# The first attention's step: two phases of scores and values in place of four, with chains laid over two steps

## The chip, the cores and the metric

The kernel runs on one core of a Trainium2 chip. The metric is the device time of one execution in microseconds (us). TensorE (PE in the rows, PEld for its weight loads), VectorE (DVE), ScalarE (ACT), GpSimd (POOL) and SyncE (SP) each run their own instruction stream and wait for each other by semaphores. TensorE writes into PSUM, eight banks of 128 partitions x 512 fp32 numbers; VectorE and ScalarE read it; GpSimd works on SBUF alone.

## What is computed

Four blocks in a row, each with a residual and a layer norm: an attention over a compressed key and value, a mixture of experts, a second attention, and two layers of local attention with a feed-forward part. The change touches only the first block:

```python
def _L0_attn_ref(x, wq, w_kv_down, w_k_up, w_v_up, wo):     # x: (4, 512, 128)
    q = jnp.einsum('bsd,qd->bsq', x, wq).reshape(B, S, H, D).transpose(0, 2, 1, 3)   # H=16, D=64
    kv_latent = jnp.einsum('bsd,ld->bsl', x, w_kv_down)     # 64 numbers a token
    k = jnp.einsum('bsl,ql->bsq', kv_latent, w_k_up)...
    v = jnp.einsum('bsl,ql->bsq', kv_latent, w_v_up)...
    q = q * cos + _rotate_half(q) * sin
    k = k * cos + _rotate_half(k) * sin
    scores = jnp.einsum('bhsd,bhtd->bhst', q, k) / jnp.sqrt(jnp.float32(D))
    scores = scores + causal
    probs = jax.nn.softmax(scores, axis=-1)
    out = jnp.einsum('bhst,bhtd->bhsd', probs, v)
    return jnp.einsum('bsq,dq->bsd', out.transpose(0, 2, 1, 3).reshape(B, S, H * D), wo)
```

All of it is fp32.

## The kernel before

`attention0` goes through 32 steps, n = 0 to 31. A step is one pair of heads (8 pairs, the outer loop) on one batch of 512 tokens (4 batches, the inner one). The first four and the last four steps are written out, the 24 between run in a hardware loop of four steps (`each`). There is no scheduler: each engine's order is the order in which its `step` function issues, and what is in flight is ordered by counting semaphores.

Within a step a *phase* p = 0 to 3 stands for one block of 128 queries, from the last (p = 0) to the first (p = 3). By causality it has (4 - p) x 128 keys, `width(p)`: 512, 384, 256 and 128. j = 0, 1 is the head of the pair. In a phase:

- `scores` (TensorE, L478): one product for each head, K = 64 rows of queries, written to one of three rotating PSUM banks 1 to 3. An fp32 product is run as two passes, so two heads are four matmuls in the trace; the two heads lie on different rows of the array and run side by side.
- `rowmax` (VectorE, L382): mask, copy to `prob` and row minimum of the negated scores, then `exp` (ScalarE, L305) in place, with the row sum in `den`.
- `turn_p` (TensorE, L488): (4 - p) transposes for each head, into bank 4 (head 0) and bank 5 (head 1), then `copy_pT`: VectorE (L388) copies bank 4 and ScalarE (L311) copies bank 5 into `probT`. A copy is as wide as its phase.
- `values` (TensorE, L500): `lat` (the latents, 64 columns) times `probT`, accumulated into `o_ps`, bank 6; the two heads lie on different columns of the array.

Once a step there is also: `project` for w = 0, 1 (TensorE, L457: the next step's queries and keys, into bank 0), `rope` for each (VectorE, L369 and L372), `rope_sum` for each (GpSimd, L265), `turn_qk` for each (TensorE, L468, bank 0) and `copy_qkT` (ScalarE, L298), whose results the next step's `scores` read. And for the step before: `copy_o` (ScalarE, L316), `reciprocal` (VectorE), `widen` (GpSimd, L271), `spread` (TensorE, L511, turns the reciprocals into bank 7), `normalise` (VectorE, L399), `output` (TensorE, L518, bank 7) and `add_y` (VectorE, L405).

TensorE thus changes between three shapes of products in every phase: 64 rows x 128 columns (scores), 128 x 64 (values) and 128 x 128 (all others; the rows of the trace show them as `64*128`, `128*64` and `128*128`).

Of the kernel before, what the change touches and what calls it, by code (L numbers as in the profile page):

```python
# [129 lines left out]
def attention0(nc, ctx, io, keep):  # L130
# [34 lines left out]
    prob = sb("prob", [P, 4, S])  # L165
    probT = sb("probT", [P, 2, S])
# [27 lines left out]
    pT_mm = sem("pT_mm")  # L194
    pT_ev = [sem(f"pT_ev{j}") for j in range(2)]
    o_mm = sem("o_mm")
# [32 lines left out]
    def score_ps(b, p, j):  # L229

        return ps[:, 1 + (NU * b + 2 * p + j) % 3, :]
# [27 lines left out]
    def _(pool):  # L259
# [31 lines left out]
    def _(act):  # L291
# [65 lines left out]
    def _(dve):  # L357
# [6 lines left out]
        def rope(n, w):  # L364
            h = HD0 // 2
            src = qk_ps.rearrange("p (t g d) -> p t g d", t=TPB, d=HD0)
# [46 lines left out]
        def step(n, b, final):  # L413
# [3 lines left out]
            if later(n):  # L417
                copy_pT(n - 1, 3)
# [8 lines left out]
            if not final:  # L427
                rope(n + 1, 1)
# [2548 lines left out]
```

## Time and profile before

| | us |
|---|---|
| three runs before, median (lowest, highest) | 1637.8 (1637.06, 1641.13) |
| the profiled execution: its own time | 1635.31 |
| its span | 1633.2 |
| step 0 begins (first scores) | 22.70 |
| step 1 begins | 40.47 |
| step 31 begins | 435.38 |
| PE busy over the span | 1504.0 |
| DVE, ACT, POOL busy over the span | 1146.4, 1087.7, 523.0 |

The profiled execution lies 2.5 us under the median of the runs, and 2.1 us of its time lie outside its span. The first attention takes about the first 454 us of the 1633. A step of it repeats every 13.18 us inside the loop. A busy time of PE is the time in which some matmul is in flight; matmuls are pipelined, so the starts of two groups tell more than their lengths.

### The profile page before, as it was taken

The page shows a single profiled execution, that of the slowest core. Times are in us where ns is not written, and L with a number is a line of the kernel's source. Part 1 is how long each engine was busy: PE and PEld are TensorE (multiplying, and loading weights), DVE is VectorE, ACT ScalarE, POOL GpSimd, SP SyncE. Part 2 cuts the span into 40 slices and gives each one's busy share as a digit, 9 for nine tenths or more (in the row PEclk, how much of TensorE's full clock was granted, in tenths as well). Part 3 has the DMA queues.
Part 4 walks back from the last instruction along what each step waited for, and adds up shares of the span by engine and source line. Part 5 has one row for each costly group of instructions (what it writes and reads, how often), then busy time and mean ns, then how long its engine had stood idle before and what let it go on. Part 6 is the DMA issues. An engine that isn't in the chain of part 4 may idle for free. (4 is left out here: it accounts for less than half of the span.)

```text
span 1633.2 us, 30449 instructions
## 1 busy us (share of the span) xinstructions
PE 1504.0 (92%) x9934; PEld 1018.6 (62%) x9934; DVE 1146.4 (70%) x2592; ACT 1087.7 (67%) x2499; POOL 523.0 (32%) x476
## 2 busy tenths in 40 slices
PE   7999999999979999999998999997999988999986
PEld 6777777777657888888863333333666655566654
DVE  2677777676657777777787888864777753777755
ACT  3565665656567888888865777754778754787852
POOL 1222222222231122221110000014777733677732
PEclk9999999999979999999997999977999998999998
DMA  7000000000002212212100000000000000000000
GB/s 244 2 2 1 0 0 0 0 0 0 1 28 80 78 64 77 76 52 77 65 1 1 1 1 1 1 1 0 2 1 1 1 1 0 1 2 1 1 1 26
DMA packets 18849, 36.54 MB, mean 22 GB/s; under 512 B 5492, under 2 KB 10736, under 8 KB 16560
## 3 DMA queue, kind: packets, MB, share of 16 engines
q1 hardware_dynamic: 18752, 35.29, 6.4%
q8 instruction: 56, 0.92, 0.2%
q14 instruction: 41, 0.34, 0.1%
HBM read 34.10 MB, written 1.18 MB: 22 GB/s over the span
## 5 line engine op out<-in xcount | busy, mean ns | idle before, releaser
L915 DVE TENSOR_TENSOR m_hidp<-m_hid,m_hidp 128x512 fp32r<-128x512 f32 x256 | 178.2, 722 | 77.9 <-ACT m_hidp L831 76.6
L305 ACT ACTIVATE a_prob<-a_prob,a_negmax 128x512 f32<-128x512 f32 (+3 forms) x256 | 142.2, 556 | 135.9 <-DVE a_negmax L382 135.9
L836 ACT ACTIVATE m_hid<-ps,pre_w 128x512 f32<-128x512 f32 x256 | 175.3, 685 | 63.5 <-PE ps L1064 62.7
L1064 PE MATMUL ps<-c_sb_st,m_w1p 128*128 128x512 f32 x768 | 191.4, 398 | 0.0
L1119 PE MATMUL ps<-m_hidp,m_w2p 128*128 128x512 f32 x768 | 190.0, 396 | 0.2 <-DVE m_hidp L915 0.2
L1441 ACT ACTIVATE c_sb_pT<-ps 128x512 f32<-128x512 f32 x256 | 137.4, 601 | 70.7 <-PE ps L1654 69.7
L265 POOL TENSOR_TENSOR a_qk_r<-a_qk_c,a_qk_s 128x512 f32<-128x512 f32 x64 | 81.6, 1275 | 318.6 <-DVE a_qk_s L372 318.6
L1511 DVE TENSOR_REDUCE c_sb_negmax<-ps 128x1 f32<-128x512 f32 x240 | 152.5, 685 | 38.9 <-PE ps L1639 38.9
L1064 PEld LDWEIGHTS ps<-c_sb_st,m_w1p 128*128 128x128 f32 x768 | 144.7, 189 | 37.9 <-issue 3.0
L1119 PEld LDWEIGHTS ps<-m_hidp,m_w2p 128*128 128x128 f32 x768 | 144.1, 188 | 35.8 <-DVE m_hidp L915 0.4
L2038 ACT ACTIVATE l_sb_prob<-ps,l_sb_negmax,l_sb_rn 128x192 f32<-128x192 f32 (+1 forms) x256 | 124.1, 499 | 47.9 <-DVE l_sb_negmax L2140 47.9
L831 ACT ACTIVATE m_hidp<-m_hid 128x512 fp32r<-128x512 f32 x256 | 153.9, 630 | 0.0
L382 DVE CUSTOM_DVE_ANT_0 a_prob<-ps,a_cmask 128x512 f32<-128x512 f32 (+3 forms) x256 | 116.6, 486 | 24.1 <-PE ps L478 23.4
L1949 POOL TENSOR_TENSOR c_sb_pT<-c_sb_pT,l_sb_tab_s 128x512 f32<-128x512 f32 x64 | 110.5, 1748 | 19.6 <-ACT c_sb_pT L1996 16.8
L388 DVE COPY a_probT<-ps 128x512 f32<-128x512 f32 (+3 forms) x128 | 61.2, 478 | 78.9 <-PE ps L488 78.9
L500 PE MATMUL ps<-a_probT,a_lat 128*64 128x128 f32 x1280 | 98.2, 282 | 19.7 <-issue 17.2
L500 PEld LDWEIGHTS ps<-a_probT,a_lat 128*64 128x64 f32 x1280 | 68.3, 136 | 76.4 <-issue 47.6
L478 PE MATMUL ps<-a_qkT 64*128 64x256 f32 (+3 forms) x512 | 104.6, 485 | 1.1 <-ACT a_qkT L298 1.1
L488 PE MATMUL ps<-keep_ident,a_prob 128*128 128x128 f32 x640 | 96.1, 281 | 0.0
L1639 PE MATMUL ps<-c_sb_st 32*128 32x512 f32 x240 | 83.5, 518 | 10.4 <-ACT c_sb_pT L1441 10.4
L2135 DVE TENSOR_REDUCE ps<-ps 128x2 f32<-128x384 f32 (+1 forms) x128 | 67.4, 526 | 33.1 <-PE ps L2267 33.1
L759 POOL CAST m_w1p<-pre_w 128x512 fp32r<-128x512 f32 x16 | 9.8, 612 | 244.8 <-DMA pre_w<-w1T 181.0
(246 smaller groups left out, 3198.5 us busy)
## 6 DMA issues: line engine op xcount, KB each, us to landing
m_gate_all<-m_gates_d SPq DMA_DIRECT2D x16, 1024.0 KB, 4.6
pre_w<-w1T SPq DMA_DIRECT2D x14, 258.0 KB, 2.7
pre_w<-w2T SPq DMA_DIRECT2D x14, 256.0 KB, 2.8
pre_wqkv<-wqkv SPq DMA_DIRECT2D x2, 768.0 KB
keep_x<-x SPq DMA_DIRECT2D x1, 1024.0 KB, 9.4
out<-keep_x SPq DMA_DIRECT2D x4, 256.0 KB, 2.3
keep_xT<-xT SPq DMA_DIRECT2D x1, 768.0 KB, 6.8
pre_m_w<-l_w SPq DMA_DIRECT2D x2, 341.0 KB
```

Of the source, the lines that this page charges most:

```text
L305: nc.scalar.activation(prob[:, u % 4, 0:width(p)], prob[:, u % 4, 0:width(p)], ACT.Exp, scale=-1.0, bias=negmax[:, u:u + 1], accum_out=den ...
L382: nc.vector.tensor_tensor_reduce(prob[:, u % 4, 0:width(p)], score_ps(b, p, j)[:, 0:width(p)], cmask[:, S - width(p):S], 1.0, HUGE, ALU.ad ...
L500: ins = nc.tensor.matmul(o_ps[64 * j:64 * j + 64, i * P:(i + 1) * P], lat[:, b * TPB + t, :], probT[:, j, t * P:(t + 1) * P], start=(t == ...
L831: nc.scalar.activation(hidp[:, c % 2, 0, f, :], hid[:, c % 2, f, :], ACT.Copy).then_inc(high_done, 1)
L836: nc.scalar.activation(hid[:, c % 2, f, :], ps[:, f, :], ACT.Gelu, bias=w1[:, k, FF + f:FF + f + 1]).then_inc(gelu_done, 1)
L915: nc.vector.tensor_tensor(hidp[:, c % 2, 1, f, :], hid[:, c % 2, f, :], hidp[:, c % 2, 0, f, :], ALU.subtract).then_inc(low_done, 1)
L1064: ins = nc.tensor.matmul(ps[:, f, :], w1p[:, k, a, f * P:(f + 1) * P], xp[:, b, c, :], start=(i == 0), stop=(i == 2))
L1119: ins = nc.tensor.matmul(ps[:, 4 + c % 2, :], w2p[:, k, a, f, :], hidp[:, c % 2, b, f, :], start=(f == 0 and i == 0), stop=(f == FB - 1 an ...
L1441: nc.scalar.activation(pT[:, m % 2, g + i, t, :], ps[:, pair(exp_turn(e)).start + i, :], ACT.Exp, scale=SCALE).then_inc(exp_done, 1)
L1511: nc.vector.tensor_reduce(negmax[:, m % 2, t, g + i:g + i + 1], ps[:, pair(max_turn(k)).start + i, :], AX.X, ALU.max, negate=True).then_in ...
L1949: ins = nc.gpsimd.tensor_tensor(qk_s[:, :, :].rearrange("p w (g d) -> p w g d", d=HD2)[:, :, :, a:a + h], raw[:, :, :, h - a:2 * h - a], t ...
L2038: ins = nc.scalar.activation(prob[:, k % 2, keys(t, i)], ps[:, 2 + k % 2, keys(t, i)], ACT.Exp, bias=negmax[:, u:u + 1], scale=rn[:, t, u: ...
```

## The change

Two phases are put together where there were four. Phases 0 and 2 (512 and 256 keys) make one, phases 1 and 3 (384 and 128 keys, together the 512 columns of a bank) the other. TensorE now issues scores 0 and 2 back to back, then the values 0 and 2 of the step before, the turned probabilities 1 and 3 of the step before, both projections, scores 1 and 3, and the values 1 and 3 of the step before. The turned probabilities of a step are copied in five full banks instead of eight pieces: VectorE copies two (`copy_wide`, `copy_mix`), ScalarE three (`copy_wide`, `copy_mix`, and `copy_tail`, which holds phase 2 of both heads). All values of a step are now taken in the next step, `add_y` comes two steps later, and both projections have a bank of their own (0 and 7). `prob` and `probT` are split in two tiles each, with more room. The number of products, transposes, exponentials and rowmaxes is as before.

```diff
@@ -226,9 +231,48 @@
         return (TPB - p) * P
-    def score_ps(b, p, j):
-        return ps[:, 1 + (NU * b + 2 * p + j) % 3, :]
+    def two_on(n):
+        return not isinstance(n, int) or n > 1
+    def turn_of(p, j):
+        return {0: 0, 2: 2, 1: 4, 3: 6}[p] + j
+    def score_ps(p, j):
+        if p == 2:
+            return ps[:, 3 - 3 * j, 0:width(2)]
+        c = 0 if p == 0 else (p // 2) * width(1)
+        return ps[:, 1 + j, c:c + width(p)]
+    def prob_of(p, j):
+        if p % 2 == 0:
+            c = (p // 2) * S
+            return prob_a[:, j, c:c + width(p)]
+        c = (p // 2) * width(1)
+        return prob_b[:, j, c:c + width(p)]
+    def turned_ps(p, j):
+        if p == 2:
+            return ps[:, 3, j * 256:(j + 1) * 256]
+        c = 0 if p == 0 else (p // 2) * width(1)
+        return ps[:, 4 + j, c:c + width(p)]
+    def probT_of(p, j):
+        if p == 2:
+            return probT_a[:, 2, j * 256:(j + 1) * 256]
+        if p == 0:
+            return probT_a[:, j, :]
+        c = (p // 2) * width(1)
+        return probT_b[:, j, c:c + width(p)]
+    def proj_ps(w):
+        return m_ps if w else qk_ps
     @block.sync
     def _(sp):
...
@@ -277,11 +321,10 @@
         pool.wait_ge(ones_set, 1)
         def step(n, b, final):
-            if not final:
-                rope_sum(n + 1, 0)
             if later(n):
                 widen(n - 1)
             if not final:
+                rope_sum(n + 1, 0)
                 rope_sum(n + 1, 1)
         each(pool, step)
...
@@ -320,37 +371,34 @@
         def step(n, b, final):
             exp(n, b, 0, 0)
+            exp(n, b, 0, 1)
+            exp(n, b, 2, 0)
+            exp(n, b, 2, 1)
             if later(n):
-                copy_pT(n - 1, 3)
-            exp(n, b, 0, 1)
-            if not later(n):
+                copy_mix(n - 1)
+            else:
                 act.wait_ge(lat_mm, 1)
                 nc.scalar.activation(lat[:, :, :], ps[:, 4:6, :].rearrange("p a (t l) -> p (a t) l", l=LAT), ACT.Copy
                                      ).then_inc(lat_ev, 1)
                 act.wait_ge(set_mm, 2)
                 nc.scalar.activation(wvo[:, :, :], ps[:, 6:8, :].rearrange("p a (h n) -> p (a h) n", n=P),
                                      ACT.Copy).then_inc(set_ev, 1)
-            exp(n, b, 1, 0)
             if later(n):
                 copy_o(n - 1)
-            exp(n, b, 1, 1)
-            copy_pT(n, 0)
-            exp(n, b, 2, 0)
-            exp(n, b, 2, 1)
-            copy_pT(n, 1)
             if not final:
                 copy_qkT(n + 1, b + 1, 0)
+            exp(n, b, 1, 0)
+            copy_wide(n)
+            if not final:
+                copy_qkT(n + 1, b + 1, 1)
+            exp(n, b, 1, 1)
+            copy_tail(n)
             exp(n, b, 3, 0)
             exp(n, b, 3, 1)
-            if not final:
-                copy_qkT(n + 1, b + 1, 1)
-            copy_pT(n, 2)
         each(act, step)
-        copy_pT(NI - 1, 3)
+        copy_mix(NI - 1)
         copy_o(NI - 1)
     @block.vector
...
@@ -411,37 +462,31 @@
         dve.wait_ge(const_ld, 32)
         def step(n, b, final):
-            before = (b - 1) % NB
-            rowmax(n, b, 0, 0)
-            rowmax(n, b, 0, 1)
+            if two_on(n):
+                add_y(n - 2, (b - 2) % NB)
+            rowmax(n, 0, 0)
+            rowmax(n, 0, 1)
+            rowmax(n, 2, 0)
+            rowmax(n, 2, 1)
             if later(n):
-                copy_pT(n - 1, 3)
+                reciprocal(n - 1, (b - 1) % NB)
+                copy_mix(n - 1)
             if not final:
                 rope(n + 1, 0)
-            rowmax(n, b, 1, 0)
-            rowmax(n, b, 1, 1)
-            if later(n):
-                reciprocal(n - 1, before)
-            copy_pT(n, 0)
-            if not final:
                 rope(n + 1, 1)
-            rowmax(n, b, 2, 0)
-            rowmax(n, b, 2, 1)
-            copy_pT(n, 1)
+            rowmax(n, 1, 0)
+            rowmax(n, 1, 1)
+            copy_wide(n)
             if later(n):
                 normalise(n - 1)
-            rowmax(n, b, 3, 0)
-            rowmax(n, b, 3, 1)
-            copy_pT(n, 2)
-            if later(n):
-                add_y(n - 1, before)
+            rowmax(n, 3, 0)
+            rowmax(n, 3, 1)
         each(dve, step)
-        copy_pT(NI - 1, 3)
+        add_y(NI - 2, NB - 2)
         reciprocal(NI - 1, NB - 1)
+        copy_mix(NI - 1)
         normalise(NI - 1)
         add_y(NI - 1, NB - 1)
@@ -449,18 +494,17 @@
     def _(pe):
         def project(n, b, w):
             if w:
-                pe.wait_ge(rope_mul, 2 * n + 1)
+                wait_past(pe, y_add, n - 2)
             else:
-                wait_past(pe, qkT_ev, 2 * n)
+                wait_past(pe, max_done, NU * (n - 1) + 4)
             h = n // NB
             for t in range(TPB):
-                ins = nc.tensor.matmul(qk_ps[:, t * P:(t + 1) * P], xT[:, b, t * P:(t + 1) * P],
+                ins = nc.tensor.matmul(proj_ps(w)[:, t * P:(t + 1) * P], xT[:, b, t * P:(t + 1) * P],
                                        wqk[:, bass.ds(h, 1), w * P:(w + 1) * P].rearrange("p a n -> p (a n)"),
                                        start=True, stop=True)
             ins.then_inc(qk_mm, 1)
         def turn_qk(n, w):
-            pe.wait_ge(rope_mul, 2 * n + 2)
             pe.wait_ge(rope_add, 2 * n + w + 1)
             if w:
                 pe.wait_ge(qkT_ev, 2 * n + 1)
@@ -470,43 +514,66 @@
         def scores(n, b, p):
             i = TPB - 1 - p
-            wait_past(pe, max_done, NU * n + 2 * p - (0 if b == 0 and p == 0 else 1))
             if p == 0:
                 pe.wait_ge(qkT_ev, 2 * n + 2)
+                wait_past(pe, max_done, NU * n)
+            if p == 2:
+                wait_past(pe, tail_ev, n)
+            if p == 1:
+                pe.wait_ge(max_done, NU * n + 2)
             for j in range(2):
                 r = slice(64 * j, 64 * j + 64)
-                nc.tensor.matmul(score_ps(b, p, j)[:, 0:width(p)], qkT[r, b % 2, 0, i * P:(i + 1) * P],
+                nc.tensor.matmul(score_ps(p, j), qkT[r, b % 2, 0, i * P:(i + 1) * P],
                                  qkT[r, b % 2, 1, 0:width(p)], start=True, stop=True, skip_group_check=True
                                  ).then_inc(s_mm, 1)
-        def turn_p(n, p):
+        def turn(n, p, j):
+            pe.wait_ge(exp_done, NU * n + turn_of(p, j) + 1)
+            for t in range(TPB - p):
+                ins = nc.tensor.transpose(turned_ps(p, j)[:, t * P:(t + 1) * P],
+                                          prob_of(p, j)[:, t * P:(t + 1) * P], ident[:, :])
+            return ins
+        def turn_wide(n):
             for j in range(2):
-                u = 2 * p + j
-                pe.wait_ge(exp_done, NU * n + u + 1)
-                wait_past(pe, pT_ev[j], 4 * n + p)
-                for t in range(TPB - p):
-                    ins = nc.tensor.transpose(ps[:, 4 + j, t * P:(t + 1) * P], prob[:, u % 4, t * P:(t + 1) * P],
-                                              ident[:, :])
-                ins.then_inc(pT_mm, 1)
+                wait_past(pe, pT_ev[j], 2 * n)
+                turn(n, 0, j).then_inc(pT_wide, 1)
+        def turn_tail(n):
+            turn(n, 2, 0)
+            turn(n, 2, 1).then_inc(pT_tail, 1)
+        def turn_mix(n):
+            for j in range(2):
+                pe.wait_ge(pT_ev[j], 2 * n + 1)
+                turn(n, 1, j)
+                turn(n, 3, j).then_inc(pT_mix, 1)
         def values(n, b, p):
             i = TPB - 1 - p
-            for j in range(2):
-                pe.wait_ge(pT_ev[j], 4 * n + p + 1)
             if p == 0:
                 wait_past(pe, o_ev, n)
+                for j in range(2):
+                    pe.wait_ge(pT_ev[j], 2 * n + 1)
+            if p == 2:
+                pe.wait_ge(tail_ev, n + 1)
+            if p == 1:
+                for j in range(2):
+                    pe.wait_ge(pT_ev[j], 2 * n + 2)
             for t in range(i + 1):
                 for j in range(2):
                     ins = nc.tensor.matmul(o_ps[64 * j:64 * j + 64, i * P:(i + 1) * P], lat[:, b * TPB + t, :],
-                                           probT[:, j, t * P:(t + 1) * P], start=(t == 0), stop=(t == i),
+                                           probT_of(p, j)[:, t * P:(t + 1) * P], start=(t == 0), stop=(t == i),
                                            skip_group_check=True)
             if p == 3:
                 ins.then_inc(o_mm, 1)
-        def spread(n):
+        def spread(n, projected):
             pe.wait_ge(r_wide, n + 1)
             wait_past(pe, y_add, n)
+            if projected:
+                pe.wait_ge(rope_mul, 2 * n + 6)
             for t in range(TPB):
                 ins = nc.tensor.transpose(m_ps[:, t * P:(t + 1) * P], rden_x[:, t * P:(t + 1) * P], ident[:, :])
             ins.then_inc(r_mm, 1)
@@ -558,47 +625,47 @@
         def step(n, b, final):
             scores(n, b, 0)
+            scores(n, b, 2)
             if later(n):
+                values(n - 1, (b - 1) % NB, 0)
                 values(n - 1, (b - 1) % NB, 2)
-                turn_p(n - 1, 3)
+                turn_mix(n - 1)
             else:
                 latents(3)
+                pe.wait_ge(rope_mul, 2)
                 value_weights()
             if not final:
                 project(n + 1, (b + 1) % NB, 0)
+                if not later(n):
+                    pe.wait_ge(set_ev, 2)
+                project(n + 1, (b + 1) % NB, 1)
             scores(n, b, 1)
+            scores(n, b, 3)
             if later(n):
+                values(n - 1, (b - 1) % NB, 1)
                 values(n - 1, (b - 1) % NB, 3)
             else:
                 pe.wait_ge(lat_ev, 1)
-            turn_p(n, 0)
-            if not final:
-                project(n + 1, (b + 1) % NB, 1)
-            scores(n, b, 2)
-            if isinstance(n, int) and n == 0:
-                pe.wait_ge(set_ev, 2)
-            values(n, b, 0)
-            turn_p(n, 1)
             if not final:
                 turn_qk(n + 1, 0)
+            turn_wide(n)
             if later(n):
-                spread(n - 1)
-            scores(n, b, 3)
-            values(n, b, 1)
+                spread(n - 1, not final)
             if not final:
                 turn_qk(n + 1, 1)
+            turn_tail(n)
             if later(n):
                 output(n - 1)
-            turn_p(n, 2)
         each(pe, step)
+        values(NI - 1, NB - 1, 0)
         values(NI - 1, NB - 1, 2)
-        turn_p(NI - 1, 3)
+        turn_mix(NI - 1)
+        values(NI - 1, NB - 1, 1)
         values(NI - 1, NB - 1, 3)
-        spread(NI - 1)
+        spread(NI - 1, False)
         output(NI - 1)
```

The first place is TensorE from scores 0 on, in a step that is written out (L numbers are those of each file). Before:

```order
L478 MATMUL ps<-a_qkT 128x512 x2
L500 MATMUL ps<-a_probT,a_lat 64x128 x4
L488 MATMUL ps<-keep_ident,a_prob 128x128 x2
L457 MATMUL ps<-a_wqk,keep_xT 128x128 x4
L478 MATMUL ps<-a_qkT 128x384 x2
L500 MATMUL ps<-a_probT,a_lat 64x128 x2
L488 MATMUL ps<-keep_ident,a_prob 128x128 x8
L457 MATMUL ps<-a_wqk,keep_xT 128x128 x4
L478 MATMUL ps<-a_qkT 128x256 x2
L500 MATMUL ps<-a_probT,a_lat 64x128 x8
```

In the change the same stretch reads (L526 are scores, L565 values, L533 turned probabilities, L502 projections, L512 turned queries and keys, L578 the spread reciprocals, L585 the output):

```order
L526 MATMUL ps<-a_qkT 128x512 x2
L526 MATMUL ps<-a_qkT 128x256 x2
L565 MATMUL ps<-a_probT_a,a_lat 64x128 x12
L533 MATMUL ps<-keep_ident,a_prob_b 128x128 x8
L502 MATMUL ps<-a_wqk,keep_xT 128x128 x8
L526 MATMUL ps<-a_qkT 128x384 x2
L526 MATMUL ps<-a_qkT 128x128 x2
L565 MATMUL ps<-a_probT_b,a_lat 64x128 x8
L512 MATMUL ps<-keep_ident,a_qk_r 128x128 x4
L533 MATMUL ps<-keep_ident,a_prob_a 128x128 x8
L578 MATMUL ps<-keep_ident,a_rden_x 128x128 x4
L512 MATMUL ps<-keep_ident,a_qk_r 128x128 x4
```

Scores and values now stand in two groups a step, and no values of the running step are left in it.

The second place is ScalarE over one step that is written out. Before (L305 exponentials, L316 `copy_o`, L311 turned probabilities, L298 queries and keys):

```order
L305 ACTIVATE a_prob,a_den<-a_prob,a_negmax 128x512
L305 ACTIVATE a_prob,a_den<-a_prob,a_negmax 128x384
L316 ACTIVATE a_o_sb<-ps 128x512
L305 ACTIVATE a_prob,a_den<-a_prob,a_negmax 128x384
L311 ACTIVATE a_probT<-ps 128x512
L305 ACTIVATE a_prob,a_den<-a_prob,a_negmax 128x256 x2
L311 ACTIVATE a_probT<-ps 128x384
L298 ACTIVATE a_qkT<-ps 128x512
L305 ACTIVATE a_prob,a_den<-a_prob,a_negmax 128x128 x2
L298 ACTIVATE a_qkT<-ps 128x512
L311 ACTIVATE a_probT<-ps 128x256
```

And in the change (L348 exponentials, L362 `copy_mix`, L367 `copy_o`, L341 queries and keys, L354 `copy_wide`, L358 `copy_tail`):

```order
L348 ACTIVATE a_prob_a,a_den<-a_prob_a,a_negmax 128x512 x2
L348 ACTIVATE a_prob_a,a_den<-a_prob_a,a_negmax 128x256 x2
L362 ACTIVATE a_probT_b<-ps 128x512
L367 ACTIVATE a_o_sb<-ps 128x512
L341 ACTIVATE a_qkT<-ps 128x512
L348 ACTIVATE a_prob_b,a_den<-a_prob_b,a_negmax 128x384
L354 ACTIVATE a_probT_a<-ps 128x512
L341 ACTIVATE a_qkT<-ps 128x512
L348 ACTIVATE a_prob_b,a_den<-a_prob_b,a_negmax 128x384
L358 ACTIVATE a_probT_a<-ps 128x512
L348 ACTIVATE a_prob_b,a_den<-a_prob_b,a_negmax 128x128 x2
```

Behind the exponentials of phases 0 and 2, `copy_o` of the step before now stands ahead of everything else that ScalarE has to do in the step.

## Rows read from the trace of the kernel before

**Rows 1.** Windows: stretch, length, busy time of each engine (instructions), clock, DMA.
```profile
40.47:435.38 394.91, 377.68 (x3361) 285.92 (x3361) 277.64 (x869) 237.86 (x690) 106.53 (x90) 1.00 0.00 1
22.70:40.47 17.77, 16.99 (x126) 13.05 (x127) 7.68 (x25) 8.98 (x23) 2.56 (x2) 1.00 0.62 215
```

**Rows 2.** Timeline of PE, one step: start, length, line, out<-in, xcount, idle.
```profile
211.56 1.13 PE L478 MATMUL ps<-a_qkT 64*128 64x512 f32 x4
212.62 0.66 PE L500 MATMUL ps<-a_probT,a_lat 128*64 128x128 f32 x8
213.21 0.44 PE L488 MATMUL ps<-keep_ident,a_prob 128*128 128x128 f32 x2
213.48 1.06 PE L457 MATMUL ps<-a_wqk,keep_xT 128*128 x8
214.47 0.92 PE L478 MATMUL ps<-a_qkT 64*128 64x384 f32 x4
215.31 0.44 PE L500 MATMUL ps<-a_probT,a_lat 128*64 128x128 f32 x4
215.68 1.09 PE L488 MATMUL ps<-keep_ident,a_prob 128*128 128x128 f32 x8
216.61 1.06 PE L457 MATMUL ps<-a_wqk,keep_xT 128*128 x8
217.60 0.70 PE L478 MATMUL ps<-a_qkT 64*128 64x256 f32 x4
218.89 1.09 PE L500 MATMUL ps<-a_probT,a_lat 128*64 128x128 f32 x16 [0.59 <-issue]
219.92 0.88 PE L488 MATMUL ps<-keep_ident,a_prob 128*128 128x128 f32 x6
220.63 0.60 PE L468 MATMUL ps<-keep_ident,a_qk_r 128*128 128x128 f32 x4
221.07 0.60 PE L511 MATMUL ps<-keep_ident,a_rden_x 128*128 128x128 f32 x4
221.60 0.49 PE L478 MATMUL ps<-a_qkT 64*128 64x128 f32 x4
222.02 0.88 PE L500 MATMUL ps<-a_probT,a_lat 128*64 128x128 f32 x12
222.82 0.66 PE L468 MATMUL ps<-keep_ident,a_qk_r 128*128 128x128 f32 x4
223.32 1.06 PE L518 MATMUL ps<-a_wvo,a_oT 128*128 x8
224.21 0.60 PE L488 MATMUL ps<-keep_ident,a_prob 128*128 128x128 f32 x4
224.74 1.13 PE L478 MATMUL ps<-a_qkT 64*128 64x512 f32 x4
```

**Rows 3.** Timeline of PE at 212.27 to 212.5: second pass of two.
```profile
212.09 0.59 PE L478 MATMUL ps<-a_qkT 64*128 64x512 f32 x2
```

**Rows 4.** Timeline of all engines in the same step, single instructions.
```profile
212.87 0.69 DVE L382 CUSTOM_DVE_ANT_0 a_prob<-ps,a_cmask 128x512 f32<-128x512 f32 x1 [0.40 <-PE ps L478]
...
216.52 0.62 ACT L305 ACTIVATE a_prob<-a_prob,a_negmax 128x384 f32<-128x384 f32 x1 [1.24 <-DVE a_negmax L382]
...
217.70 0.69 DVE L369 TENSOR_TENSOR a_qk_c<-ps,a_cos 128x512 f32<-128x512 f32 x1
...
218.21 0.58 ACT L311 ACTIVATE a_probT<-ps 128x512 f32<-128x512 f32 x1
...
218.31 0.75 DVE L372 TENSOR_TENSOR a_qk_s<-ps,a_sin 128x256 f32<-128x256 f32 x2
...
219.14 1.28 POOL L265 TENSOR_TENSOR a_qk_r<-a_qk_c,a_qk_s 128x512 f32<-128x512 f32 x1 [0.69 <-DVE a_qk_s L372]
...
220.50 0.56 DVE L388 COPY a_probT<-ps 128x384 f32<-128x384 f32 x1 [0.76 <-PE ps L488]
...
221.27 0.60 ACT L298 ACTIVATE a_qkT<-ps 128x512 f32<-128x512 f32 x1
```

More of the change, by code:

```diff
@@ L164, in attention0 @@
     rden_x = sb("rden_x", [P, S])
-    prob = sb("prob", [P, 4, S])
-    probT = sb("probT", [P, 2, S])
+    prob_a = sb("prob_a", [P, 2, S + S // 2])
+    prob_b = sb("prob_b", [P, 2, S])
+    probT_a = sb("probT_a", [P, 3, S])
+    probT_b = sb("probT_b", [P, 2, S])
     o_sb = sb("o_sb", [P, S])
@@ L193, in attention0 @@
     exp_done = sem("exp_done")
-    pT_mm = sem("pT_mm")
+    pT_wide = sem("pT_wide")
+    pT_tail = sem("pT_tail")
+    pT_mix = sem("pT_mix")
     pT_ev = [sem(f"pT_ev{j}") for j in range(2)]
+    tail_ev = sem("tail_ev")
     o_mm = sem("o_mm")
@@ L300, in exp, with copy_wide, copy_tail, copy_mix @@
         def exp(n, b, p, j):
-            i, u = TPB - 1 - p, 2 * p + j
-            act.wait_ge(max_done, NU * n + u + 1)
-            if u == 0:
+            i, k = TPB - 1 - p, turn_of(p, j)
+            act.wait_ge(max_done, NU * n + k + 1)
+            if k == 0:
                 wait_past(act, recip, n - 1)
-            nc.scalar.activation(prob[:, u % 4, 0:width(p)], prob[:, u % 4, 0:width(p)], ACT.Exp,
-                                 scale=-1.0, bias=negmax[:, u:u + 1],
+            nc.scalar.activation(prob_of(p, j), prob_of(p, j), ACT.Exp,
+                                 scale=-1.0, bias=negmax[:, 2 * p + j:2 * p + j + 1],
                                  accum_out=den[:, b % 2, 2 * i + j:2 * i + j + 1]).then_inc(exp_done, 1)
-        def copy_pT(n, p):
-            act.wait_ge(pT_mm, NU * n + 2 * p + 2)
-            nc.scalar.activation(probT[:, 1, 0:width(p)], ps[:, 5, 0:width(p)], ACT.Copy).then_inc(pT_ev[1], 1)
+        def copy_wide(n):
+            act.wait_ge(pT_wide, 2 * n + 2)
+            nc.scalar.activation(probT_a[:, 1, :], ps[:, 5, :], ACT.Copy).then_inc(pT_ev[1], 1)
+        def copy_tail(n):
+            act.wait_ge(pT_tail, n + 1)
+            nc.scalar.activation(probT_a[:, 2, :], ps[:, 3, :], ACT.Copy).then_inc(tail_ev, 1)
+        def copy_mix(n):
+            act.wait_ge(pT_mix, 2 * n + 2)
+            nc.scalar.activation(probT_b[:, 1, :], ps[:, 5, :], ACT.Copy).then_inc(pT_ev[1], 1)
         def copy_o(n):
@@ L365, in rope @@
             h = HD0 // 2
[L366 removed]
+            src = proj_ps(w).rearrange("p (t g d) -> p t g d", t=TPB, d=HD0)
             dve.wait_ge(qk_mm, 2 * n + w + 1)
@@ L376, in rope, with rowmax, copy_wide, copy_mix @@
             ins.then_inc(rope_mul, 1)
-        def rowmax(n, b, p, j):
-            u = 2 * p + j
-            dve.wait_ge(s_mm, NU * n + u + 1)
+        def rowmax(n, p, j):
+            dve.wait_ge(s_mm, NU * n + turn_of(3 if p == 1 else p, j) + 1)
             dve.sem_inc(s_held, 1)
-            nc.vector.tensor_tensor_reduce(prob[:, u % 4, 0:width(p)], score_ps(b, p, j)[:, 0:width(p)],
+            nc.vector.tensor_tensor_reduce(prob_of(p, j), score_ps(p, j),
                                            cmask[:, S - width(p):S], 1.0, HUGE, ALU.add, ALU.min,
-                                           negmax[:, u:u + 1]).then_inc(max_done, 1)
-        def copy_pT(n, p):
-            dve.wait_ge(pT_mm, NU * n + 2 * p + 1)
-            nc.vector.tensor_copy(probT[:, 0, 0:width(p)], ps[:, 4, 0:width(p)]).then_inc(pT_ev[0], 1)
+                                           negmax[:, 2 * p + j:2 * p + j + 1]).then_inc(max_done, 1)
+        def copy_wide(n):
+            dve.wait_ge(pT_wide, 2 * n + 1)
+            nc.vector.tensor_copy(probT_a[:, 0, :], ps[:, 4, :]).then_inc(pT_ev[0], 1)
+        def copy_mix(n):
+            dve.wait_ge(pT_mix, 2 * n + 1)
+            nc.vector.tensor_copy(probT_b[:, 0, :], ps[:, 4, :]).then_inc(pT_ev[0], 1)
         def reciprocal(n, b):
@@ L402, in add_y @@
             dve.wait_ge(y_mm, n + 1)
-            wait_past(dve, y_add, n - NB + 1)
+            wait_past(dve, y_add, n)
             ts = slice(b * TPB, (b + 1) * TPB)
```

1 line of the change is left out of this document (removed).

## Prediction

> **What bounds the kernel now.** I read the trace in four views. First the windows: from the start of step 1 to the start of step 31 lie 394.91 us, so 30 steps at a mean of 13.16 us. In them PE is busy 377.68 us, DVE 277.64, ACT 237.86 and POOL 106.53 at a granted clock of 1.00 [rows 1], or 12.6, 9.3, 7.9 and 3.6 us a step. TensorE is the engine that is nearly full. But its busy time says nothing on how well it is used, since matmuls overlap; that needs the timeline of one step [rows 2], where the start of a group to the start of the next is what the group costs. The reader is to see two things there.
>
> First, one real wait. Scores of phase 2 (217.60) are followed by values of phase 0 at 218.89, 1.29 us later, with "idle 0.59". By the fixed and running costs below the scores need 0.64 us, so TensorE waits 0.65 us. It waits for ScalarE's copy of the turned probabilities, which starts at 218.21 and takes 0.58, to 218.79 [rows 4].
>
> Second, fixed costs at each change of shape. Scores cost 1.06, 0.84 and 0.42 us for 512, 384 and 128 columns: 0.21 for each 128 and 0.21 fixed. The second pass of scores 0 starts at 212.09 [rows 3], 0.53 after the first; 0.43 of that are its columns, 0.10 is the change of weights between passes. So 0.11 lies at the change to values. Values cost 0.37, 0.59, 0.80 and 1.03 us for one to four blocks: 0.22 for each and 0.15 fixed. Eight projection matmuls ahead of scores cost 0.99 (213.48 to 214.47), the eight of the output, ahead of a product of their own shape, 0.89 (223.32 to 224.21): 0.10 for the change into scores. Four transposes ahead of scores cost 0.53, so 0.108 each; eight behind values cost 0.93, 0.07 more than eight times that. One round of scores, values, turning thus has 0.10 + 0.11 + 0.15 + 0.06 = 0.42 us in which nothing is computed, and there are four rounds a step [rows 2].
>
> **The change part by part.** *Removed on TensorE: two rounds of four.* Scores 2 stand right behind scores 0, and scores 3 behind scores 1. Each merge takes away 0.42 us. It leaves one new cost: a scores group that follows another loads new weights on the same rows, which is what happens between the two passes of one group, 0.10 us [rows 3]. Bounds: nothing, if that load hides, and 0.21, the whole fixed part of a scores group [rows 2], if the merge keeps all of it. I take 0.10, since it is the same act. So 2 x (0.42 - 0.10) = 0.64 us a step.
>
> *A rule on that load.* The trace has 0.10 us between two passes whose weights go to the same rows [rows 3]. The Trainium skill ("TensorE: Matmul & The Clock Gate", the section "Part 2: What happens when you issue a matmul") says that the queue pulls a weight load ahead of running matmuls if the row groups don't conflict or the load goes to the background buffer. By the second half of that rule the new load would hide, and the step would come to 11.74 us where the row gives 11.94. Here the trace speaks against the rule.
>
> *Removed: the wait at values 0.* In the change all values of a step are taken in the next. The copies they read end long before, as laid out below. That is 0.65 us a step.
>
> *Moved: everything else on TensorE.* No product is added. The step laid out by the costs above, from scores 0 at 0: scores 2 at 1.05, values 0 and 2 at 1.7, turned 1 and 3 at 3.1, projections at 4.1 and 5.0, scores 1 at 5.9, scores 3 at 6.8, values 1 and 3 at 7.2, turned queries 8.2, turned 0 at 8.7, spread 9.6, turned keys 10.0, turned 2 at 10.4, output 10.9, end 11.9. Now each hand-over against it.
>
> (a) *Scores to probabilities.* The first rowmax starts 1.31 us after scores 0 (212.87 [rows 4] against 211.56 [rows 2]). Four rowmaxes, at 0.69 each although two are half as wide, end by 4.07. Projection 0, which overwrites the bank of the last of them, stands at 4.1. `add_y`, ahead of them on VectorE, ends by 0.8, and projection 1, which now waits for it because of their common bank, stands at 5.0.
> (b) *Projection to the next scores.* Projection 0 ends at 5.0, rope 0 starts 0.3 later (estimate by the 0.35 from the end of the columns, 212.09 + 0.43, to the rowmax at 212.87 [rows 3, 4]) and takes 0.69 + 0.75 [rows 4], so to 6.7; rope 1 to 8.2. POOL's `widen`, now first in its queue, can start at 4.1 and is out of the way. POOL's sum takes 1.28 [rows 4]: to 8.0 and to 9.4. TensorE needs them at 8.2 and 10.0. In hand 0.2 and 0.6.
> (c) *ScalarE.* It waits for the values 1 and 3 (end 8.1), since `copy_o` stands ahead. Behind it are `copy_o` 0.58, queries 0.60, exponential 0.62, `copy_wide` 0.58, keys 0.60 [rows 4]: 2.98 at most, to 11.3, where the next scores need the keys at 11.9. In hand 0.6. The queries' copy itself has to end ahead of the turned keys at 10.0: 8.3 + 1.18 = 9.5, in hand 0.5. Then exponential and `copy_tail` to 12.5; scores 2 need its bank at 13.0, in hand 0.5. Two narrow exponentials to 13.3; turned 1 and 3 need them at 15.
> (d) *Normalising.* Spread ends at 10.0, DVE starts 0.2 later (turned 1, first head, to copy: 219.92 + 3 x 0.108 = 220.24, the copy starts 220.50 [rows 2, 4]) and takes 0.69 as the ropes' products do: 10.9. TensorE is there at 10.9. This one has nothing in hand; I take 0.05 us of waiting.
> (e) *Copies.* One full copy of 0.6 replaces two on DVE (384 columns are 0.56 [rows 4]); ScalarE's sum stays. DVE's 9.3 us fall, and it stays far under 11.9, so this is worth nothing by itself; it is cover for (a) to (d).
>
> The step: 13.18 - 0.65 - 0.64 + 0.05 = 11.94 us. Against the mean of 13.16, 30 steps give 36.6 us. Step 0 (22.70 to 40.47, 17.77 us, [rows 1]) also holds the setup. In it `project` 1 now waits for ScalarE's copy of the value weights, and the first turned queries wait for the POOL sum, but the waits at values 0 and at the end are gone; laid out the same way I get a gain of 2.2 us, an estimate with bounds 0 and 4. The last step has the same products in other places; I take nothing, with 1 us either way. Sum: 38.8 us. The profiled 1635.31 becomes 1596.5, and the median 1637.8 becomes 1599.0, all the rest of the program being untouched.
>
> **Rivals.** *A (0.62): as above,* TensorE back to back but for little: 1594 to 1605.
> *B (0.12): the second scores' weights load for free,* the weight unit has only to be ready by the end of the group before. 0.20 us a step less, 6 us: 1593. For it: only that the second group is another product, with weights of its own. Against: the 0.10 between passes [rows 3]. This is what the rule of the Trainium skill named above would give.
> *C (0.18): a hand-over without cover takes part of it back.* (b) has 0.2 in hand and (d) none, both through estimates of latencies; at 0.2 to 0.6 us of new wait a step it costs 6 to 18 us: 1605 to 1617. For it: five single instructions in a row on ScalarE, three on POOL. Against: busy times of 60% to 80% of the step.
> *D (0.04): the change does not do what it says.* Fixed costs come at each group whatever its neighbour, so only the waiting goes, and (d) and (c) bring half a microsecond or more: within 5 us of 1637.8.
> *E (0.04): slower, by ScalarE's chain (c).* `copy_o` waits for the values of the step before and holds up the keys that the next scores need. It decides the step when it is 0.6 us longer than its rows say, and the step is longer than 13.16 when it is 0.6 + 1.2 = 1.8 us longer, 4.8 in place of 3.0. At 2.0 us longer the step would be 13.4 and the time 1643. Against: the same five instructions take 0.58 to 0.62 in this trace whatever runs beside them.
>
> **How the numbers follow.** The number is A's. The range runs from 1589 (B with the better bounds of step 0 and the last step) to 1615 (most of C); outside are D, E and the worst of C, about 1 in 10 to 2 in 10. Case A alone has 1594 to 1605. A time within 0.3% (5 us) is about what a measurement of this kernel can't tell from no change. A, B and C are faster by more, 0.92, and so is a quarter of D: 0.93. The rest of D is within: 0.03. E is slower: 0.04.
>
> **What the changed profile would show.** The step at 11.9 to 12.0 us between scores 0 groups. Scores 2 starting 1.05 after scores 0 if the reload costs 0.10, and 0.95 if it is free. Values 0 and 2 with no idle ahead. Output starting within 0.1 of the end of turned 2. On ScalarE an idle stretch of about 3 us ahead of `copy_o`, waiting for PE; then none up to the last exponential. POOL's sums as long as before. What would make it wrong: idle time on PE ahead of turned queries or keys, released by POOL (C, hand-over b), ahead of scores 0 or 2, released by ScalarE (c), or ahead of the output, released by DVE (d).

## The result and the profile after

The changed kernel takes 1593.82 us (median of 4 runs, 1590.51 to 1601.03) against 1638.49 us before (4 runs), a ratio of 0.973 (95% interval 0.970 to 0.976), 44.7 us less. The prediction was 1599.0, with a range of 1589 to 1615. The profiled executions stand at 1591.31 and 1635.31, 44.0 us apart.

The same windows as [rows 1] in the profile of the change: step 1 to step 31, then the time up to step 0, step 0, and the last step with the end of the block (length, busy time of PE, PEld, DVE, ACT, POOL with their instructions, granted clock, DMA).

```profile
37.87:392.76 354.89, 354.29 (x3360) 293.25 (x3361) 265.19 (x809) 231.57 (x663) 106.93 (x90) 1.00 0.00 1
0.00:25.07 25.07, 14.48 (x53) 11.27 (x53) 3.54 (x8) 3.50 (x4) 2.93 (x7) 1.00 0.95 278
25.07:37.87 12.80, 11.78 (x92) 8.73 (x92) 6.77 (x23) 6.53 (x16) 2.55 (x2) 1.00 0.68 235
392.76:411.50 18.74, 14.59 (x149) 11.52 (x148) 9.57 (x29) 8.74 (x27) 2.51 (x7) 0.97 0.01 1
```

Thirty steps take 354.89 us where they took 394.91 [rows 1]: 40.0 us of the 44.0, or 11.83 a step in place of 13.16. Step 0 gave 5.0 (17.77 to 12.80), of which 2.4 went back because its first scores came later (25.07 in place of 22.70, the first weights having landed later: VectorE's first instruction waits for them until 8.42 us in this profile and until 6.05 in the one before). From the start of step 31 to the last `add_y` it is 16.7 us where it was 17.9, another 1.2; the last 0.2 lie outside these stretches. VectorE is busy 12.5 us less over the thirty steps, 0.41 a step, and ScalarE 0.21.

One step on TensorE, the counterpart of [rows 2] (start, length, xcount; L526 scores, L565 values, L533 turned probabilities, L502 projections, L512 turned queries and keys, L578 spread, L585 output):

```profile
215.44 1.56 PE L526 MATMUL ps<-a_qkT 64*128 64x512 f32 x8
216.93 1.53 PE L565 MATMUL ps<-a_probT_a,a_lat 128*64 128x128 f32 x24
218.39 1.09 PE L533 MATMUL ps<-keep_ident,a_prob_b 128*128 128x128 f32 x8
219.32 1.95 PE L502 MATMUL ps<-a_wqk,keep_xT 128*128 x16
221.20 1.14 PE L526 MATMUL ps<-a_qkT 64*128 64x384 f32 x8
222.27 1.09 PE L565 MATMUL ps<-a_probT_b,a_lat 128*64 128x128 f32 x16
223.35 0.65 PE L512 MATMUL ps<-keep_ident,a_qk_r 128*128 128x128 f32 x4
223.84 1.04 PE L533 MATMUL ps<-keep_ident,a_prob_a 128*128 128x128 f32 x8
224.71 0.60 PE L578 MATMUL ps<-keep_ident,a_rden_x 128*128 128x128 f32 x4
225.15 0.60 PE L512 MATMUL ps<-keep_ident,a_qk_r 128*128 128x128 f32 x4
225.58 0.60 PE L533 MATMUL ps<-keep_ident,a_prob_a 128*128 128x128 f32 x4
226.24 1.15 PE L585 MATMUL ps<-a_wvo,a_oT 128*128 x8
227.32 0.70 PE L526 MATMUL ps<-a_qkT 64*128 64x512 f32 x2
```

The reader is to compare starts. Scores 0 and 2 together last from 215.44 to 216.93, 1.49 us. Apart, in [rows 2], scores 0 took 1.06, and 256 columns cost 0.64 by the prediction's figures, so 1.70. The four transposes at 225.58 are followed by the output only 0.66 later; their columns are worth 0.44. That is the one new wait of any size. Groups of one shape that follow each other cost no more than their columns: turned 0 to spread 0.87 for eight transposes, spread to turned keys 0.44 for four.

The passes of scores 0 and 2, from three narrow windows of the same timeline, the counterpart of [rows 3]:

```profile
215.97 0.60 PE L526 MATMUL ps<-a_qkT 64*128 64x512 f32 x2
```

```profile
216.40 0.38 PE L526 MATMUL ps<-a_qkT 64*128 64x256 f32 x2
```

```profile
216.62 0.38 PE L526 MATMUL ps<-a_qkT 64*128 64x256 f32 x2
```

The first pass of scores 0 takes 0.53 as before (0.43 of columns). The second takes 0.43, columns alone, and the first pass of scores 2 takes 0.22, again columns alone (0.21). Only the first pass of the whole group costs 0.10 more. Scores 2 thus start 0.96 behind scores 0; the prediction had written 0.95 for a load that is free and 1.05 for one that is not.

### The profile page after: what moved, and what is told of

Its sections match the earlier page's. It is cut to its first block and busy times, and to the rows that moved or that the text cites. A ratio compares the mean times of both kernels' runs of the same rounds, so it can differ in the third digit from the quotient of the medians.

```text
span 1589.3 us, 29947 instructions
## 1 busy us (share of the span) xinstructions
PE 1475.6 (93%) x9934; PEld 1023.1 (64%) x9934; DVE 1133.2 (71%) x2528; ACT 1079.8 (68%) x2467; POOL 521.9 (33%) x476
## 5 line engine op out<-in xcount | busy, mean ns | idle before, releaser
L348 ACT ACTIVATE a_prob_a<-a_prob_a,a_negmax 128x256 f32<-128x256 f32 (+1 forms) x128 | 77.2, 604 | 36.9 <-DVE a_negmax L429 36.9
L315 POOL TENSOR_TENSOR a_rden_x<-a_rden,a_ones 128x512 f32<-128x512 f32 x32 | 33.4, 1043 | 199.5 <-DVE a_rden L444 199.5
L526 PE MATMUL ps<-a_qkT 64*128 64x384 f32 (+3 forms) x512 | 87.9, 462 | 1.1 <-ACT a_qkT L341 1.1
L429 DVE CUSTOM_DVE_ANT_0 a_prob_a<-ps,a_cmask 128x256 f32<-128x256 f32 (+1 forms) x128 | 63.7, 554 | 25.3 <-PE ps L526 25.3
L367 ACT ACTIVATE a_o_sb<-ps 128x512 f32<-128x512 f32 x32 | 19.1, 598 | 90.3 <-PE ps L565 90.3
L1743 PE MATMUL ps<-c_sb_pT,c_sb_v 128*32 128x512 f32 x512 | 76.3, 673 | 0.0
L502 PE MATMUL ps<-a_wqk,keep_xT 128*128 (+1 forms) x512 | 65.0, 281 | 10.3 <-DVE a_wqk L407 8.7
```

The lines of the kernel that those rows point to most:

```text
L526: nc.tensor.matmul(score_ps(p, j), qkT[r, b % 2, 0, i * P:(i + 1) * P], qkT[r, b % 2, 1, 0:width(p)], start=True, stop=True, skip_group_ch ...
```

## The experiments

"Step" is the mean interval of 16 steps in the hardware loop, by VectorE's `add_y`: 13.18 us before, 11.86 in the change. The kernel before took 1637.3 us beside e1 to e4 and 1637.4 beside e5 to e7 (medians). The interval of medians is less sharp than the step, since the rest of the program moved by itself from profile to profile (last section).

| kernel | median us | ratio to before (95%) | step us |
|---|---|---|---|
| change | 1593.8 | 0.973 (0.970 to 0.976) | 11.86 |
| e1, four rounds again | 1614.1 | 0.987 (0.985 to 0.988) | 12.50 |
| e2, spread earlier | 1584.3 | 0.968 (0.967 to 0.970) | 11.58 |
| e3, before with one swap | 1621.9 | 0.990 (0.989 to 0.992) | 12.59 |
| e4, one more copy on ScalarE | 1595.8 | 0.973 (0.971 to 0.975) | 11.86 |
| e5, three more | 1615.7 | 0.987 (0.985 to 0.989) | 12.56 |
| e6, turning split | 1585.6 | 0.968 (0.966 to 0.969) | 11.61 |
| e7, one more copy on VectorE | 1598.0 | 0.976 (0.973 to 0.978) | 11.89 |

**e1: what is a round worth?** The change with the merges on TensorE undone and everything else kept.

```diff
             scores(n, b, 0)
-            scores(n, b, 2)
             if later(n):
                 values(n - 1, (b - 1) % NB, 0)
+            scores(n, b, 2)
+            if later(n):
                 values(n - 1, (b - 1) % NB, 2)
...
             scores(n, b, 1)
-            scores(n, b, 3)
             if later(n):
                 values(n - 1, (b - 1) % NB, 1)
+            scores(n, b, 3)
+            if later(n):
                 values(n - 1, (b - 1) % NB, 3)
```

> The changed kernel, but TensorE issues scores 0, values 0, scores 2, values 2 and scores 1, values 1, scores 3, values 3: four rounds again, all waits, copies and tiles as in the change. Theory A (each change of shape costs, and each first product behind one exposes its weight load): a split adds, by the trace of the change, 0.09 + 0.10 (into scores) and 0.09 + 0.05 (into values), 0.34 us, so 0.67 us a step over 31 steps: 21 us more than the change, about 1614. Theory B (as the prediction had it, the 0.10 inside scores is a reload that merging keeps): 0.16 a split, 10 us more, about 1604. Theory C (the order by itself costs nothing, the gain is the wait that went): as the change, about 1594.

Measured: 1614.1, the step 0.65 longer than the change's (theory A: 0.67). TensorE's timeline, and the second pass of scores 2 from a narrow window:

```profile
204.07 0.70 PE L526 MATMUL ps<-a_qkT 64*128 64x256 f32 x4
204.71 0.66 PE L565 MATMUL ps<-a_probT_a,a_lat 128*64 128x128 f32 x8
205.29 1.09 PE L533 MATMUL ps<-keep_ident,a_prob_b 128*128 128x128 f32 x8
```

```profile
204.39 0.38 PE L526 MATMUL ps<-a_qkT 64*128 64x256 f32 x2
```

With values 0 ahead of it, the first pass of scores 2 takes 0.32 (204.07 to 204.39); in the change the same pass took 0.22. So the 0.10 belongs to the first product after a change of shape, and not to a change of weights on the same rows. Theory B, the prediction's own, falls. The two alternations really cost 0.70: e1 no longer has the wait of 0.05 ahead of the turned queries that the change has (hand-over (b) below); its last block of values is followed by them after 0.37 us (210.18 to 210.55), as one block costs by [rows 2].

**e3: what was the wait worth?** The kernel before, with two calls of ScalarE exchanged.

```diff
-            exp(n, b, 1, 1)
             copy_pT(n, 0)
+            exp(n, b, 1, 1)
```

> The kernel before, with one thing changed on ScalarE: the copy of the turned phase 0 ahead of the second exponential of phase 1. Theory A (the 0.65 us at values 0 is ScalarE's order alone): values 0 start 0.6 us earlier and nothing behind takes it back, 31 x 0.6, 18 us less than before, about 1620. Theory B (the exponential that now comes later holds up the turned phase 1): the wait moves by one group, 1632 to 1640.

Measured: 1621.9, the step 0.59 shorter than before. ScalarE and TensorE in its timeline:

```profile
210.42 0.70 PE L478 MATMUL ps<-a_qkT 64*128 64x256 f32 x4
...
210.44 0.58 ACT L311 ACTIVATE a_probT<-ps 128x512 f32<-128x512 f32 x1
...
210.92 0.61 ACT L305 ACTIVATE a_prob<-a_prob,a_negmax 128x384 f32<-128x384 f32 x1
...
211.12 1.09 PE L500 MATMUL ps<-a_probT,a_lat 128*64 128x128 f32 x16
...
212.15 0.55 PE L488 MATMUL ps<-keep_ident,a_prob 128*128 128x128 f32 x3
```

Values 0 now start 0.70 behind scores 2 where they started 1.29 behind [rows 2]; 0.06 of the wait is left. The exponential that was put back ends by 211.5, before the turned phase 1 at 212.15 needs it. So the order of two instructions on ScalarE was worth 15 us, a third of the change's gain, without touching anything else.

**e2 and e6: the wait for normalising.** e2 puts `spread` ahead of `turn_wide` on TensorE and `normalise` ahead of `copy_wide` on VectorE.

```diff
-            copy_wide(n)
             if later(n):
                 normalise(n - 1)
+            copy_wide(n)
...
-            turn_wide(n)
             if later(n):
                 spread(n - 1, not final)
+            turn_wide(n)
```

> The changed kernel with the spread reciprocals ahead of the turned phase 0 on TensorE, and normalising ahead of the full-bank copy on VectorE. Theory A (in the loop TensorE waits about 0.3 us a step for normalising, and nothing else is as tight): the output product starts without a gap, 24 to 30 steps x 0.3 us, 7 to 9 us less than the change, about 1586. Theory B (the wait moves: the later copies of phase 0 delay the keys or the next scores): within 3 us of the change, 1591 to 1597, with idle time ahead of the turned keys or scores 0.

Measured: 1584.3, the step 0.28 shorter. On TensorE:

```profile
205.44 0.66 PE L512 MATMUL ps<-keep_ident,a_qk_r 128*128 128x128 f32 x4
205.94 0.60 PE L578 MATMUL ps<-keep_ident,a_rden_x 128*128 128x128 f32 x4
206.37 1.04 PE L533 MATMUL ps<-keep_ident,a_prob_a 128*128 128x128 f32 x8
207.25 0.60 PE L512 MATMUL ps<-keep_ident,a_qk_r 128*128 128x128 f32 x4
207.68 0.60 PE L533 MATMUL ps<-keep_ident,a_prob_a 128*128 128x128 f32 x4
208.12 1.06 PE L585 MATMUL ps<-a_wvo,a_oT 128*128 x8
209.11 0.70 PE L526 MATMUL ps<-a_qkT 64*128 64x512 f32 x2
```

The output starts 0.44 behind the turned phase 2, with no gap, and takes 0.99 where it took 1.08. The weight loads say why. In e2 the load for the output's first product starts 0.11 ahead of that product, under the transposes (208.01 against 208.12); in the change it waits too, and the two start together (226.23 and 226.24). From e2, then from the change:

```profile
208.01 0.97 PEld L585 LDWEIGHTS ps<-a_wvo,a_oT 128*128 128x128 f32 x8
```

```profile
226.23 0.19 PEld L585 LDWEIGHTS ps<-a_wvo,a_oT 128*128 128x128 f32 x1 [0.29 <-issue]
```

So a product that had waited also exposes its weights' load. Theory A.

e6 reaches the same from the other side: one head of `turn_wide` ahead of the turned queries, the other behind the spread.

```diff
+            wait_past(pe, pT_ev[0], 2 * n)
+            turn(n, 0, 0).then_inc(pT_wide, 1)
             if not final:
                 turn_qk(n + 1, 0)
-            turn_wide(n)
             if later(n):
                 spread(n - 1, not final)
+            wait_past(pe, pT_ev[1], 2 * n)
+            turn(n, 0, 1).then_inc(pT_wide, 1)
```

> The changed kernel with head 0 of the turned phase 0 ahead of the turned queries, then the spread reciprocals, then head 1; VectorE as in the change. Theory A (TensorE waits 0.055 us for the POOL sum ahead of the turned queries and 0.3 for normalising ahead of the output, and both waits go): step 11.5, 9 us less than the change, about 1584. Theory B (the keys' chain on ScalarE, 0.5 us later now, takes it back): 1590 to 1597.

Measured: 1585.6, step 11.61. Both waits go, and a small one appears, as theory B has it in kind but not in size: the turned keys start 0.50 (211.22 to 211.72) behind four transposes that are worth 0.44, since ScalarE's copy of the queries ends at 211.58.

```profile
211.22 0.60 PE L533 MATMUL ps<-keep_ident,a_prob_a 128*128 128x128 f32 x4
211.72 0.63 PE L512 MATMUL ps<-keep_ident,a_qk_r 128*128 128x128 f32 x4
```

**e4 and e5: how much has ScalarE's chain in hand?** More full-bank copies ahead of `copy_o`, one in e4 and three in e5, into a tile that nobody reads.

```diff
         def copy_o(n):
             act.wait_ge(o_mm, n + 1)
+            for _ in range(1):        # 3 in e5
+                nc.scalar.activation(o_dump[:, _, :], o_ps, ACT.Copy)
```

> The changed kernel with one more full-bank copy (into a tile that nobody reads) on ScalarE ahead of the copy of o, 0.48 us more in the chain from the values to the next keys. Theory A (the chain has 0.5 us or more in hand): within 3 us of the change, 1591 to 1597. Theory B (the chain is what sets the step in the change): 31 x 0.48 = 15 us more, about 1609.

> The changed kernel with three more full-bank copies (into a tile that nobody reads) on ScalarE ahead of the copy of o: 3 x 0.48 = 1.44 us more in the chain. Theory A (the trace of the change has 0.5 us in hand from the copy of the queries to the turned keys, 0.9 from the keys to the next scores): 0.9 us a step longer, 31 x 0.9 = 28 us more than the change, about 1622. Theory B (the chain has so much in hand that it never decides): 1591 to 1597. Theory C (no slack at all, the run with one copy was luck): 45 us more, 1638.

Measured: e4 1595.8 and a step of 11.86, no change. e5 1615.7 and a step of 12.56, 0.70 longer. TensorE in e5:

```profile
210.84 0.60 PE L581 MATMUL ps<-keep_ident,a_rden_x 128*128 128x128 f32 x4
212.24 0.63 PE L515 MATMUL ps<-keep_ident,a_qk_r 128*128 128x128 f32 x4 [0.80 <-ACT a_qkT L342]
212.71 0.60 PE L536 MATMUL ps<-keep_ident,a_prob_a 128*128 128x128 f32 x4
213.14 1.06 PE L588 MATMUL ps<-a_wvo,a_oT 128*128 x8
```

The turned keys wait 0.96 us (1.40 from the spread, 0.44 of it columns) for ScalarE, as theory A said. But the step grows by 0.70 only: the output behind them now starts without a gap (213.14 behind 212.71), so the 0.3 us of the old wait are absorbed. Theory A had the place and missed the absorption, 28 us expected and 22 measured.

**e7: does VectorE's load count?** One more copy there, where it waits for the projection anyway.

```diff
         def copy_mix(n):
             dve.wait_ge(pT_mix, 2 * n + 1)
+            nc.vector.tensor_copy(o_dump[:, :], ps[:, 4, :])
             nc.vector.tensor_copy(probT_b[:, 0, :], ps[:, 4, :]).then_inc(pT_ev[0], 1)
```

> The changed kernel with one more full-bank copy on VectorE (into a tile that nobody reads) ahead of its copy of the turned phases 1 and 3, 0.6 us, where VectorE waits 0.73 us for the projection. Theory A (fewer copies on VectorE are worth nothing by themselves): as the change, 1591 to 1597. Theory B (VectorE's load is what the change lightened, and it counts): up to 31 x 0.6 = 18 us more, 1612.

Measured: 1598.0, just past A's bound, and a step of 11.89, so 0.03 us for an instruction that occupies 0.6. Theory A in the step; 1 us of the 4 between the medians comes from there (31 x 0.03). As much as the rest shows up behind the first attention, in code that is the same: from the last `add_y` to the end e7's profile takes 1183.8 us, the change's 1179.9. The copy stands where VectorE waits anyway. What one would cost ahead of `normalise`, where nothing is in hand, was not measured.

## Why the prediction was right, and where it was off

*What bounds the kernel.* Right: TensorE, and what it loses at changes of shape and at one wait. The wait was then measured alone, in e3, and the changes of shape, as far as they lie between scores and values, in e1.

*Removed: two rounds of four.* Right in kind, and the term that was mis-sized: 0.64 us a step predicted. The prediction split the fixed 0.21 of a scores group into 0.11 at the change to values and 0.10 "between passes", and kept the 0.10 for each merged group. The profile after and e1 show that the 0.10 is paid once, by the first product behind a change of shape. A merge therefore takes all of the prediction's own 0.42 and, beside it, the 0.10 within scores 2 (its first pass is 0.32 in e1, 0.22 in the change). That is 2 x 0.52 = 1.04.

The subtraction agrees: the step shown above is 11.88 and holds some 0.37 of waiting, so 11.51 are worked; the step before was 13.18 with 0.65 of waiting, so 12.53. The difference is 1.02. Of it, e1 gives back 0.70 by undoing the merges of scores and values. The other 0.32 belong to turning, which e1 leaves in two groups; the prediction's own figures give the same, 2 x (0.10 into the group and 0.06 in its first product), but no run isolated it. Counted in changes of shape, a step has 12 before, 10 in e1 and 6 in the change; 1.02 / 6 is 0.17 us each and 0.70 / 4 is 0.175. It was rival B's cause at more than B's size: 0.20 was foreseen, 0.4 measured, because the 0.10 inside scores 2 goes as well.

*The rule on the load.* The Trainium skill ("TensorE: Matmul & The Clock Gate", "Part 2: What happens when you issue a matmul") lets a weight load run ahead of matmuls in flight. Within the merged group the trace agrees, with passes of 0.43 and 0.22. Behind a change of shape the load shows, 0.10. The Trainium skill ("TensorEngine Tiling (Array Packing)", "Tiling Modes", under its key properties) states that changing the mode drains TensorE. The traces agree in so far as every change of shape costs time and groups of one shape do not; that it is the drain which costs, no run separates. The price here is 0.35 us for a change into scores and back to values (e1: 0.70 for two).

*Removed: the wait at values 0.* Right. 0.65 predicted, 0.59 by e3 (which leaves 0.06), and in the change no idle time ahead of values.

*Hand-over (d), normalising.* Right in place, wrong in size: 0.05 us predicted with "nothing in hand". The output starts 0.66 behind the turned phase 2 instead of 0.44, 0.22 of waiting, and its first product is 0.10 longer for having waited. e2 gets back 0.28. The two sides themselves ran as laid out. The prediction had 1.3 us from the spread to VectorE's end as well as to TensorE's turn; the trace has 1.33 (224.71 to 225.35 + 0.69 = 226.04) and 1.31 (224.71 to 226.02). What the sum put at nothing is the time from VectorE's end to TensorE's start. In the hardware loop it is 0.14 to 0.20 us (226.04 to 226.24 in this step), in the steps that are written out 0.05. In step 1, written out:

```profile
47.95 0.69 DVE L450 TENSOR_TENSOR a_oT<-ps,a_o_sb 128x512 f32<-128x512 f32 x1 [0.18 <-PE ps L578]
```

```profile
48.70 1.16 PE L585 MATMUL ps<-a_wvo,a_oT 128*128 128x128 f32 x8
```

And in the step shown above, in the loop:

```profile
225.35 0.69 DVE L450 TENSOR_TENSOR a_oT<-ps,a_o_sb 128x512 f32<-128x512 f32 x1 [0.18 <-PE ps L578]
```

Written out, the output waits 0.07 us, about as predicted; in the loop 0.16 to 0.22. In the loop the trace has a register instruction of TensorE's sequencer for this line in between, from 226.08 to 226.18, and written out it has none. It fits the difference; no run took it away.

*Hand-over (b), projection to scores.* 0.2 in hand predicted; in the trace the turned queries start 1.08 behind the values (222.27 to 223.35) where four blocks of values cost 1.03 before [rows 2], so 0.05 of waiting. TensorE's groups from projection 0 on are 0.12 shorter than laid out (4.03 less 0.05 in place of 4.1), POOL's sum ends 0.07 later (3.97 behind projection 0 in place of 3.9), and its end to TensorE's start takes another 0.06, which the sum put at nothing.

*Hand-over (c), ScalarE.* Right ahead of the turned keys, 0.5 in hand: e4 puts 0.48 in and nothing moves, e5 puts 1.44 in and the wait is 0.96, so 0.48 in hand. Ahead of the scores 0.6 was predicted; the keys' copy ends at 226.38 and the scores start at 227.32, so it is 0.9. No run tried that one alone. The idle stretch of "about 3 us" ahead of `copy_o` is there, 2.86:

```profile
223.41 0.60 ACT L367 ACTIVATE a_o_sb<-ps 128x512 f32<-128x512 f32 x1 [2.86 <-PE ps L565]
224.04 0.60 ACT L341 ACTIVATE a_qkT<-ps 128x512 f32<-128x512 f32 x1
```

*(e), copies.* Right as far as tested: one copy more costs 0.03 us a step where VectorE waits (e7).

*Step 0.* 2.2 us predicted, 5.0 in the profile. Most of the difference is chance: the 32 products of the value weights took 3.68 us or 1.96 us, and this varies between runs of these kernels. The granted clock is given as 1.00 for step 0 both in [rows 1] and above, but that means only that the trace has no entry there. Its first entry, at full clock, begins at 30.96 us in the profile before and at 28.01 in the change's; the products ahead of it run at about half the rate (0.115 us each of these 32, against 0.061). Before, they came ahead of it, in the change behind it:

```profile
26.61 3.68 PE L541 MATMUL ps<-a_woT,a_wv 64*64 64x128 f32 x32
```

```profile
28.99 1.96 PE L608 MATMUL ps<-a_woT,a_wv 64*64 64x128 f32 x32
```

e4, whose extra copy first comes in step 1, had the long one (its first entry begins at 32.30). Its step 0 is 38.91 - 23.24 = 15.67 us, 2.1 less than before:

```profile
23.24 2.93 PE L529 MATMUL ps<-a_qkT 64*128 64x512 f32 x8 [0.78 <-ACT a_qkT L342]
...
28.00 3.68 PE L611 MATMUL ps<-a_woT,a_wv 64*64 64x128 f32 x32
...
38.91 1.13 PE L529 MATMUL ps<-a_qkT 64*128 64x512 f32 x4 [0.41 <-ACT a_qkT L342]
```

*The sum.* 1.02 for the rounds and 0.65 for the wait, less 0.37 of new waiting, is 1.30 for the step shown, against 1.24 predicted for a loop step (13.18 to 11.94). Over thirty steps the windows give 40.0 against 36.6. The last step, taken at nothing, gave 1.2. The forecast came close because two errors pulled apart: the merges are worth 0.4 more a step (B's side), and the new waits cost 0.3 more (C's side, ahead of the output and of the turned queries, where the prediction had named them as signs of C). That they nearly cancel is luck. 1593.8 lies just below case A's own 1594 to 1605 and beside B's 1593.

## What to carry to other kernels

Count the changes of product shape on TensorE, and group products of one shape. A scores, values, turning round costs about half a microsecond here (0.52) at each of the four sizes, which is as much as some 300 columns of a scores product. When a dense order is made denser, go through the hand-overs again with the shorter times, and give each hand-over itself a time: 0.05 to 0.2 us from one engine's end to TensorE's start here. Cover of 0.2 us is not cover. Before rebuilding a schedule, look at what a single exchange in the order of the engine that is waited for gives: here a third of the gain.

## What the runs showed that I had not expected

The first product behind a change of shape or behind a wait is longer by the load of its weights: 0.10 us for scores and for the output, and this is what looked like a reload between passes. Values and transposes show it smaller, 0.05: 0.15 and 0.16 us from the first start to the second, where the next ones take 0.11.

The rest of the program, identical in all of these kernels, was not constant. From the start of the last `add_y` of the first attention to the end it took 1180.0 us before and 1179.9 in the change's profile, but 1189.4 in e4's. The granted clock of the middle part tells where: first the change, then e4.

```profile
700.00:1300.00 600.00, 546.83 (x3407) 307.21 (x3406) 443.55 (x867) 418.57 (x896) 186.09 (x178) 0.93 0.03 9
```

```profile
701.60:1301.60 600.00, 547.99 (x3362) 302.87 (x3360) 439.05 (x851) 415.48 (x891) 183.92 (x175) 0.91 0.03 9
```

The four runs of the change fit this in their order: 1590.5 and 1591.3 us at a mean granted clock of 0.961, 1596.3 at 0.960 and 1601.0 at 0.954. Only the one at 1591.3 has a trace. Inside the attention the clock was at 1.00 throughout, so the step there is the better measure of an experiment. What decides that clock was not looked into.
